# A soft mixture-of-experts and delta-rule kernel whose prologue takes turned inputs, and whose last attention ends in another order

## What is computed

```
k, q, v = x @ Wk.T, x @ Wq.T, x @ Wv.T           # 16 heads of 8
k, q = layernorm(k, kln_g, kln_b), layernorm(q, qln_g, qln_b)   # per head, over its 8 numbers
dot = (q * D**-.25) @ (k * D**-.25), causal
x1 = layernorm(x + softmax(dot) @ v @ Wo.T + bo)
x2 = layernorm(x1 + soft_moe(x1))                # logits to 8 experts x 64 slots, two softmaxes, gelu
x3 = layernorm(x2 + delta_rule_block(x2))        # 16 heads, a scan over the tokens, then a gated MLP
out = layernorm(x3 + ternary_mlp(x3))            # 128 -> 512 -> 512 -> 512 -> 128
```

## Time and profile before

| | us |
|---|---|
| median of 3 runs | 1253.74 (1253.59 to 1254.05) |
| profiled execution | 1254.35 |
| its span | 1252.6 |
| busy of the span: PE | 1120.8 |
| DVE | 936.0 |
| ScalarE | 625.2 |
| GpSimd | 444.6 |
| mean granted clock of TensorE | 0.958 |

### The profile page before, as it was taken

The page is one execution under the profiler, slowest core; times in us unless marked ns, Lnnn a source line. Parts: engine busy times, 40 slices in busy tenths (PEclk is TensorE's granted clock), DMA queues, the critical chain, the costliest instruction groups (busy, mean ns, idle before and its releaser), DMA issues.

```text
span 1252.6 us, 19130 instructions
## 1 busy us (share of the span) xinstructions
PE 1120.8 (89%) x6049; PEld 588.9 (47%) x6049; DVE 936.0 (75%) x2152; ACT 625.2 (50%) x1233; POOL 444.6 (35%) x576
## 2 busy tenths in 40 slices
PE   5989999999999999999999920589899999999997
PEld 2434455554554445644546510244545545555453
DVE  4646737757687887878987999999889898897131
ACT  1061654746737457375374611345455674565542
POOL 3041221312345154262530001453745636536310
PEclk8989999999999999999899975699999999999999
DMA  4221030221323313323212653302112022010000
GB/s 116 81 85 42 3 119 10 86 69 37 119 56 97 101 41 118 80 69 111 62 38 62 168 149 113 90 16 53 37 35 61 19 61 57 14 33 9 17 9 9
DMA packets 85107, 79.83 MB, mean 64 GB/s; under 512 B 42128, under 2 KB 62736, under 8 KB 83024
## 3 DMA queue, kind: packets, MB, share of 16 engines
q1 hardware_dynamic: 84768, 78.88, 22.6%
q10 hardware_dynamic: 272, 0.13, 0.0%
HBM read 43.17 MB, written 35.00 MB: 62 GB/s over the span
## 4 chain that ended last, share of the span: by engine, by line
PE 65%; DVE 19%; issue 7%; ACT 6%; POOL 2%; DMA 0%; ACTq 0%; SPq 0%; DVEq 0%; POOLq 0%
PE ps L1592 14%; PE ps L1573 7%; PE ps L1139 5%; PE ps L1063 5%; PE ps L1098 5%; PE ps L1108 3%; PE ps L1101 3%; PE ps L1126 3%; PE ps L1583 2%; ACT arena L1756 2%; ACT arena L1729 2%; PE ps L1216 2%; PE ps L1206 2%; DVE arena L2253 2%; PE ps L1168 2%
## 5 line engine op out<-in xcount | busy, mean ns | idle before, releaser
L2253 DVE TENSOR_REDUCE arena<-ps 128x4 f32<-128x512 f32 (+2 forms) x192 | 198.1, 1043 | 49.3 <-PE ps L1101 47.8
L1729 ACT ACTIVATE arena<-ps 128x512 f32<-128x512 f32 (+2 forms) x196 | 106.8, 567 | 221.8 <-PE ps L1063 109.9
L1592 PE MATMUL ps<-arena,late 128*128 128x512 f32 x480 | 211.5, 593 | 2.8 <-POOL arena L990 2.5
L1756 ACT ACTIVATE arena<-ps 128x1024 f32<-128x1024 f32 (+3 forms) x256 | 169.2, 711 | 32.9 <-PE ps L1126 31.6
L873 POOL TENSOR_SCALAR_AFFINE_SELECT arena<-arena 128x512 f32<-128x512 f32 x128 | 90.6, 711 | 231.2 <-ACT arena L1756 231.2
L1592 PEld LDWEIGHTS ps<-arena,late 128*128 128x128 f32 x480 | 89.6, 190 | 110.4 <-issue 103.7
L979 POOL TENSOR_TENSOR arena<-arena 128x256 f32<-128x256 f32 x128 | 93.9, 734 | 133.8 <-issue 90.2
L1950 ACT ACTIVATE arena<-ps,f_s 128x512 f32<-128x512 f32 x128 | 83.5, 688 | 104.5 <-PE ps L1592 87.7
L1108 PE MATMUL ps<-mask_qk,ident_b 128*128 128x512 bf16 x381 | 102.7, 395 | 15.5 <-DVE arena L2695 15.5
L1573 PE MATMUL ps<-arena,late 128*128 128x512 f32 x256 | 113.4, 595 | 2.8 <-ACT arena L1950 2.7
L1063 PE MATMUL ps<-ident,arena 128*128 128x128 f32 (+1 forms) x576 | 88.4, 285 | 13.8 <-ACT arena L1729 7.0
(11 more groups left out here) (237 smaller groups left out, 1890.1 us busy)
## 6 DMA issues: line engine op xcount, KB each, us to landing
qr<-q_rep SPq DMA_DIRECT2D x16, 512.0 KB, 4.0
kr<-k_rep SPq DMA_DIRECT2D x16, 512.0 KB, 4.9
scan_d<-late SPq DMA_DIRECT2D x6, 1104.0 KB
arena<-scan_d SPq DMA_DIRECT2D x12, 552.0 KB, 6.7
q_rep<-hilo SPq DMA_DIRECT2D x24, 256.0 KB, 3.0
k_rep<-hilo SPq DMA_DIRECT2D x24, 256.0 KB, 3.3
proj_d<-arena SPq DMA_DIRECT2D x8, 768.0 KB, 5.1
late<-proj_d SPq DMA_DIRECT2D x6, 768.0 KB, 4.5
```

What stands on the lines that cost most here:

```text
L1592: last = pe.matmul(ps[:, ring2.bank(f"{n}{c}"), :], w[:, k, c * P:(c + 1) * P], src[:, k, :], start=(k == 0), stop=(k == HC - 1))
L1729: return act.activation(dst, src(ps[:, bank, :]), func, **kw)
L1756: act.activation(prob[:, gg % 2, 2 * pr:2 * pr + 2, p_off[jt]:p_off[jt] + w], ps[:, bank:bank + 2, 0:w], ACT.Exp).then_inc(p_taken, 1)
L2253: v.tensor_reduce(heads[:, 2 * pr:2 * pr + 2, gs[0]:gs[-1] + 1], ps[:, at:at + 2, 0:len(gs) * w].rearrange("p q (n w) -> p q n w", w=w), X ...
```

## The change

1. The host passes four more inputs, which are only laid out anew: `x_T` (tokens of each sequence turned), `qkv_T` (the three projections turned and beside one another), `out_T`, and `qk_rows` (gains and biases of the head norms repeated for the 128 rows). PE no longer turns weights or tokens.
2. Slots 0 to 6: `transpose_x` and `take_xT` are gone. `load_xT` (SyncE, one transfer of 256 KB more for each sequence) fills `xT`, and `project_qkv` waits for it.
3. The prologue: the 87 semaphore credits, given by GpSimd alone before, are given in thirds by DVE, ScalarE and GpSimd. The four projections go to banks 0 to 3 without a pause. ScalarE squares each tile, DVE sums it (`first_norms`). `scale_four` writes every head four times, scaled by its norm (four instructions of 128x128 for each of 8 jobs, a job being a group of q or of k); PE turns them (`spread_heads`); ScalarE makes a high and a low part of a job, each with a scale and a bias by row (for 7 jobs; DVE for one), and DVE's `place_heads` joins the parts into `qr` or `kr`. This stands in the place of stores, loads and 50 of the idle matmuls. Matmuls on a tile of zeros (`blank_matmuls`, 7, 10 and 8) stand between. The last four jobs, `norm_slots` and `finish_weights` are interleaved with the 19 maxima.
4. Idle matmuls are added: 14 in slot 0, 8 in the last slot.
5. The end of the last slot on PE is reordered, with `take_x2` ahead of `take_att` on ScalarE; DVE does more of its tail behind the last head group (`advance` 2 and 5 for 4 and 3). Two idle matmuls are gone.
6. In the border, the squares of the last sequence (`square_last`, DVE) become `square_heads(B - 1)` on ScalarE, behind `make_x2`.

```
-            for j, n in enumerate(("Wq", "Wk", "Wv", "Wo")):
-                load(raw_w[:, j, :], A[f"L0_attn_{n}"], w_att)
+            load(w_qkv[:, :], A["qkv_T"], w_att)
+            load(xT, A["x_T"][0, :, :], w_att)
+            load(qk_gb[:, :], A["qk_rows"], w_gb)
             load_x(0, True)
...
+            def load_xT(b):
+                sp.dma_start(xT, A["x_T"][b, :, :]).then_inc(xT_loaded, 16)
+
             def load_x(b, first=False):
                 if not first:
+                    sp.wait_ge(f_ready, CREDIT + F.filled(f"qkv{NT - 1}", b - 1))
+                    load_xT(b)
                     sp.wait_ge(x_biased, CREDIT + b)
-                    sp.wait_ge(f_ready, CREDIT + F.filled("xT", b - 1))
...
-            replicate(0)
-            load_half(0, 0)
-            load_half(0, 1)
...
             def project_qkv(b, turn, t):
-                pe.wait_ge(f_act, CREDIT + F.emptied("xT", b))
+                pe.wait_ge(xT_loaded, CREDIT + b * 16)
...
-                if front is not None:
-                    transpose_x(front, turn)
...
+                        if front is None and moe is not None and (gg, jt) == (0, 1):
+                            idle_matmuls(3, ring.bank("L3"))
+                        if front is None and moe is not None and (gg, jt) == (0, 2):
+                            ring.wait_free(pe, "M0", *turn)
+                            idle_matmuls(5, ring.bank("M0"))
+                        if b is not None and moe is None and (gg, jt) in ((0, 2), (0, 3)):
+                            ring.wait_free(pe, "L3", *turn)
+                            idle_matmuls(4, ring.bank("L3"))
+                        if b is not None and moe is None and (gg, jt) in ((2, 2), (2, 3)):
+                            ring.wait_free(pe, "sn", *turn)
+                            idle_matmuls(3, ring.bank("sn"))
...
+                if last:
+                    expert_hidden(moe, turn, 1)
+                    turn_products(b, turn, 3)
+                    pe.wait_ge(p_taken, CREDIT + B * len(p_units))
+                    late_turn_x2(tail)
+                    transpose_att(b, turn)
+                    expert_hidden(moe, turn, 2)
+                    project_att(b, turn)
+                    expert_hidden(moe, turn, 3)
+                    return turn
...
+            for i in range(4):
+                spread_heads(i)
+            blank_matmuls(8)
             for k in range(X_LATE):
                 idle_matmuls(2)
                 scores_for_maxima(0, f"x{k}", first)
+                if 1 <= k < 5:
+                    spread_heads(3 + k)
...
+            def scale_four(i):
+                j, g, _ = spread_order[i]
+                q = 4 * HD * g + j * D
+                roots = qk_r.rearrange("p (t n) -> p t n", t=NT)[:, :, q // HD:q // HD + 4]
+                for t in range(NT):
+                    r = v.tensor_tensor(four_fold[:, i, t, :].rearrange("p (q c d) -> p q c d", c=4, d=HD),
+                                        qk[:, t, q:q + 4 * HD].rearrange("p (q d) -> p q d", d=HD).unsqueeze(2).broadcast_to([P, 4, 4, HD]),
+                                        roots[:, t, :].unsqueeze(2).unsqueeze(3).broadcast_to([P, 4, 4, HD]), ALU.mult)
+                r.then_inc(scaled_four if i < 7 else qk_normed, 1)
...
+            for i in range(4):
+                scale_four(i)
+            for i in range(4):
+                place_heads(i)
+            scale_four(4)
+            scale_four(5)
+            slots_normed = norm_slots(o)
             for k in range(X_LATE):
                 maximum(0, f"x{k}")
+                if k < 2:
+                    scale_four(6 + k)
+                if 2 <= k < 6:
+                    place_heads(k + 2)
...
+                if k == X_LATE - 2:
+                    finish_weights(o)
+                if k >= 2:
+                    advance(o, slots_normed, 1)
```

More of the change, by code:

```diff
@@ L187, in build @@
         warm = sb("warm", [P, 1])
+        blank = sb("blank", [P, P], BF16)
         ARENA = 36736
@@ L311, in build @@
         c0 = Carve(moe_at)
-        raw_w = c0.take(4, P)
         raw_slot = c0.take(4, P)
@@ L319, in build @@
         ones_zeros = c0.take(2, S)
+        rows_of = c0.take(2 * HD)
+        copy_of = c0.take(4)
+        sign = c0.take(2)
+        low_gb = c0.take(4)
+        low_of = [qk_T[:, 0, :], qk_T[:, 1, :], act_T, x1T]
+        four_fold = Carve(prob_at).take(2 * NG, NT, P)
+        high_of = [hilo[:, k // 2, k % 2, :] for k in range(4)]
         c2 = Carve()
@@ L825, in _ @@
         def _(g):
+            for x in counted[2::3]:
+                g.sem_inc(x, CREDIT)
             g.memset(ident[:, :], 0.0).then_inc(setup_pool, 1)
@@ L1269, in slot @@
                                 idle_matmuls(3, ring.bank("h0"))
-                        if b is not None and (gg, jt) == (NG, 2):
+                        if b is not None and (gg, jt) == (NG, 2) and not last:
                             if moe is not None:
@@ L1871, in slot @@
                     take_hidden(moe, 1)
+                if last:
+                    take_x2(tail)
+                    take_att(b)
+                    take_hidden(moe, 2)
+                    take_hidden(moe, 3)
+                    take_projections(tail)
+                    return
                 if b is not None:
@@ new lines, in first_norms @@
+            def first_norms():
+                o = Order(v, front_done, DVE_FRONT, 0, CREDIT)
+                for t in range(NT):
+                    v.wait_ge(tile_squared, t + 1)
+                    r = v.tensor_reduce(qk_var[:, t * 2 * NH:(t + 1) * 2 * NH], qk_sq[:, t, :].rearrange("p (g d) -> p g d", d=HD),
+                                        X, ALU.add)
+                    if t < NT - 1:
+                        r.then_inc(tile_summed, 1)
+                o.mark(r)
+                v.wait_ge(tile_summed, NT - 1)
+                o.settle()
+                o.step(v.tensor_scalar(qk_var, qk_var, RSQRT_SCALE / HD, RSQRT_SCALE * LN_EPS, ALU.mult, ALU.add))
+                rsqrt(o, qk_r, qk_var, qk_t)
+                v.wait_ge(qk_taken, 1)
+                o.end('DVE_FRONT')
@@ new lines, in place_heads @@
+            def place_heads(i):
+                j, g, bank = spread_order[i]
+                if i in by_vector:
+                    v.wait_ge(spread_ready, i + 1)
+                    for dst, gb in ((high_of[i % 4], qk_gb), (low_of[i % 4], low_gb)):
+                        v.tensor_scalar(dst, ps[:, bank, :], gb[:, 2 * j:2 * j + 1], gb[:, 2 * j + 1:2 * j + 2],
+                                        ALU.mult, ALU.add).then_inc(high_made, 1)
+                    v.wait_ge(high_made, 2 * by_vector.index(i) + 2)
+                else:
+                    v.wait_ge(parts_made, 2 * sum(n not in by_vector for n in range(i + 1)))
+                v.scalar_tensor_tensor((qr, kr)[j][:, g, :], high_of[i % 4].bitcast(F32), sign[:, j:j + 1], low_of[i % 4],
+                                       ALU.mult, ALU.add).then_inc(first_placed, 1)
@@ L2840 @@
     arrays, args = {}, {}
-    for name, value in inputs.items():
+    laid = dict(inputs)
+    laid["x_T"] = np.swapaxes(np.asarray(inputs["L0_attn_x"]), 1, 2)
+    laid["qkv_T"] = np.concatenate([np.asarray(inputs[f"L0_attn_{n}"]).T for n in ("Wq", "Wk", "Wv")], axis=1)
+    laid["out_T"] = np.asarray(inputs["L0_attn_Wo"]).T
+    laid["qk_rows"] = np.stack([np.tile(np.asarray(inputs[f"L0_attn_{n}"]), NH) for n in ("qln_g", "qln_b", "kln_g", "kln_b")], axis=1)
+    for name, value in laid.items():
         a = np.ascontiguousarray(value)
```

221 lines of the change are left out of this document (129 added, 92 removed).

## The result

| | before | changed |
|---|---|---|
| median, the runs of the result | 1253.89 us (1253.59 to 1256.16, 4) | 1245.24 us (1242.9 to 1245.9, 4) |
| ratio, 95% interval | | 0.9924 (0.991 to 0.9939) |
| span of the profiled execution | 1252.6 | 1241.2 |
| a second series (after_again) | 1256.59 (1253.15 to 1258.89, 11) | 1242.44 (1241.11 to 1245.61, 5), 0.9895 (0.9873 to 0.9916) |

The kernel is 0.8% faster, 8.7 us, where 20 were forecast; 1245.24 lies above the range. The profiled execution, 1242.9, is the best of its four, 11.4 us better in span than that of before. One execution of the kernel before, 1345.85 us in the fourth series at a granted clock of 0.825, is left out of every ratio.

A forecast was written before the change was run, and what follows sets the result against it. PE was taken to bound the slots from 287 to 610 us, DVE the last slot and border. Terms 6.5 + 7.3 + 1.4 + 0.9 + 1.8 + 2.2 = 20.1 us off 1254.35 gave 1234.2, said as 1234; range 1226 to 1244.

The forecast's parts named there:

- The prologue: x0's scores start 16 us earlier, of which 6.5 us remain after the maxima; bounds 4 (PE at half clock) and 9.
- rival 1: Idle matmuls do not hold the clock, first maxima run slow; gain only 13.3 us, time 1241; chance 0.17.
- Slot 0's clock: In slot 0, 14 idle matmuls keep the clock up; +1.4 us, from -1 to +3.
- Slots: Seven slot starts lose the transposes and the wait for bank 7's copy; 7.3 us, bounds 4 and 7.6.
- rivals 2 and 4: 2: slot starts give nothing, 1240.5 us, chance 0.07; 4: slots without transposes lose the clock, 1264 us, chance 0.04.
- Last slot: 8 idle matmuls against the half clock at 618 to 630 us; +0.9 us, from -2 to +1.3.
- The end: End of last slot: new order and earlier DVE work shorten the wait before the residual; +1.8 us, 0 to 2.5.
- Squares: Border: the last sequence's squares come off DVE whole, onto idle ScalarE; +2.2 us, 0 if they come too late.

The follow-up runs named there:

- after_again: The changed kernel run once more without an edit; 1242.44 us, 0.9895 of the kernel before.
- a_idle_x: The changed kernel with 21 more idle matmuls in the prologue, ahead of x2 to x14; 1237.46 us, 0.9853 of the kernel before.
- b_xT: The kernel before with only the turned tokens coming by a transfer, transposes and copy gone; 1249.2 us, 0.9941 of the kernel before.
- d_all: a_idle_x with 9 blank matmuls for 7, last hidden matmul before output projection, 3 idle matmuls ahead of x15 to x18 and of slots' weights; 1235.23 us.
- e_no_idle_slot0: d_all without the 14 idle matmuls of slot 0; 1235.35 us.
- c_no_idle_slot0: a_idle_x without the 14 idle matmuls of slot 0; 1238.27 us.
- d_blank9: a_idle_x with 9 blank matmuls for 7 ahead of the first projections; 1236.28 us.
- c_hidden3: a_idle_x with the last hidden matmul of the last slot put back ahead of the output projection; 1236.66 us.
- c_square_dve: a_idle_x with the squares of the last sequence back on DVE; 1238.84 us.
- c_no_idle_last: a_idle_x without the 8 idle matmuls of the last slot; 1236.92 us.
- d_three: The changed kernel with 3 idle matmuls for 2 ahead of x2 to x9, 8 more in all; 1236.75 us.

## Why the prediction was wrong

- **The failed step** is in "The prologue": "Not all 16 us remain, since DVE then has more to do between maxima." The DVE sum was right in form: it made DVE the bound and put PE's waits to nothing. But PE waited 0.48, 1.03 and 0.50 us for DVE between 29.0 and 33.2, the clock fell at 33, and from then on PE at half clock was the bound (13.77 busy of 14). "If PE runs these units at half clock" stood there as the bound of 4; the likeliest value was 6.5, measured 3.95. With the gaps filled DVE is the bound, as the sum had it, and the first attention scores come 30.4 us after x0's: with x0's scores at 21.57 that would have been a lead of 7.6, within the forecast's 4 to 9 (a_idle_x shows 9.27, 1.7 of it from its projections). So the clock cost 3.6 us here. It was rival 1 that came true, with 0.17. That its sum of 1241 lies near the profiled 1242.9 is in part luck: its last slot of -1.5 measured -0.50, and the fall at 828 was not in it.
- **Slot 0's clock**, +1.4 and 0.9 for the transposes: measured -0.30. The 0.9 is shown by no run: b_xT, with that part alone, has the slot as long as before, though with its half clock elsewhere. In the changed kernel the clock fell at 57 to 61, ahead of the 14 idle matmuls, and again at 87. With d_all's prologue ahead the slot is 1.0 to 2.5 us shorter with the 14 than without (e_no_idle_slot0); with a_idle_x's it is not (c_no_idle_slot0 gains 0.55 there, a_idle_x loses 0.31). So what they are worth depends on where the clock falls before them, and stays open, in the median too.
- **Slots**: 6.4 forecast for slots 2 to 6, 6.8 measured, and 6.8 with that part alone. Right; rivals 2 and 4 are out, the clock has no fall between 92 and 616.
- **Last slot**, +0.9: measured -0.50 in this kernel. The half clock did shrink, from 10.3 us to 3.4, and the two kernels without the 8 idle matmuls took 1.5 more in the slot than their neighbours with them; but d_blank9, which has them, took as long as those without. The sum counted from a slot that the change also moved: with the turned tokens alone the slot takes 2.8 us more than before (b_xT, one profile), so there was that to make good first.
- **The end**, +1.8: the residual did come 2.03 earlier, yet the border had only 0.82 of it. The forecast followed DVE's wait for the projection and not what PE does behind it: the tail's projections wait 0.78 for the copy of the hidden layer that was moved behind. c_hidden3 gives 1.05 back. The term was 0.8.
- **Squares**, +2.2: 2.30, and 2.32 by c_square_dve. The prediction has ScalarE idle from the squares at 716.04 until 761.97; its own row of 761.97 has a wait of 31.78, so ScalarE worked until 730.19. It did no harm, as the new squares run at 727.68.
- **The MLP's start**: 1.66 us of the lead lost, by matmuls that took 1.70 longer, to a fall at 828 to 832 that no part of the change touches. It shows in some profiles and not in others of nearly the same code (a_idle_x 823 to 827, c_no_idle_last none). Whether the shift in time or chance decides it was not settled.

Together: 2.55 + 2.6 + 1.4 + 1.0 + 1.66, less 0.4 and 0.1 to the good, are 8.7 us between 20.1 and 11.4. The remaining 2.3 between the profiled execution and the median go with a lower mean clock: 0.959 in the profiled one, 0.954 and 0.955 in the other three, which left no trace. The profile of after_again, also at 0.954, has the prologue's fall 3.4 us longer and that of 57 nearly 7.

## What to carry to other kernels

When a change moves the bound from the engine with a clock to another, price the waits it leaves there: here three waits of 0.5 to 1.0 us, close together, stood ahead of 14 us at half clock, and the bound came back at half speed. Where extra work is put between an engine's steps, see what keeps the other one busy in the gaps; here 8 idle matmuls more took 3.9 us off the stretch from x0's scores to the first attention scores (d_three). And when one operation is taken from ahead of a wait by putting it behind, look for the next user of its result before counting the gain.
